# Block softmax: the running maximum's scan between the slot's last two block sums, and GpSimd's low parts subtracted in two halves

## The reference, cut to what matters

```python
def step(carry, kv):
    o, m, l = carry
    kj, vj = kv
    s = jnp.einsum('bhnqd,bhkd->bhnqk', qb, kj) * scale
    m_new = jnp.maximum(m, s.max(axis=-1))
    p = jnp.exp(s - m_new[..., None])
    alpha = jnp.exp(m - m_new)
    l_new = alpha * l + p.sum(axis=-1)
    o_new = (alpha[..., None] * o + jnp.einsum('bhnqk,bhkd->bhnqd', p, vj)) / l_new[..., None]
    return ((o_new, m_new, l_new), None)
```

## Time and profile before

| what | value |
|---|---|
| median of 3 runs | 2512.51 us |
| lowest, highest | 2512.49, 2518.15 us |
| the profiled execution: span from first to last instruction | 2524.1 us |
| TensorE busy | 2303.2 us (91%) |
| VectorE busy | 2215.7 us (88%) |
| ScalarE busy | 1658.7 us (66%) |
| GpSimd busy | 1477.1 us (59%) |

### The profile page before, as it was taken

One profiled execution on the slowest core, in us unless ns is written; L12 is line 12 of the kernel. 1 busy time (PEld: TensorE's weight loads), 2 busy tenths in 40 slices (PEclk: granted clock), 3 DMA queues, 4 the chain that ended last, 5 costly groups with the idle time before them and its releaser, 6 DMA issues. The chain is left out here.

```text
span 2524.1 us, 44143 instructions
## 1 busy us (share of the span) xinstructions
PE 2303.2 (91%) x14954; PEld 1763.9 (70%) x14954; DVE 2215.7 (88%) x4723; ACT 1658.7 (66%) x2901; POOL 1477.1 (59%) x1073
## 2 busy tenths in 40 slices
PE   5996699659999999999999999999999999957995
PEld 3553588537777777777777777777777777746884
DVE  6675688789999999999999999999999999956886
ACT  2464344367777777787877778777777887733443
POOL 1145344336667666667667767666876766653442
PEclk8997799879999999999999999999999999978997
DMA  8811566564344533444223332233322333006665
GB/s 202 228 63 49 172 211 208 170 167 118 85 97 102 131 94 84 101 112 105 63 62 87 92 86 62 62 79 79 99 71 63 79 86 72 5 27 190 205 212 187
DMA packets 169680, 281.89 MB, mean 112 GB/s; under 512 B 32972, under 2 KB 122962, under 8 KB 169456
## 3 DMA queue, kind: packets, MB, share of 16 engines
q1 hardware_dynamic: 160240, 260.11, 39.9%
q0 software_dynamic: 9216, 18.96, 2.2%
HBM read 118.94 MB, written 62.39 MB: 72 GB/s over the span
## 5 line engine op out<-in xcount | busy, mean ns | idle before, releaser
L2628 POOL TENSOR_TENSOR b_prob<-b_prob,b_weight 128x1024 f32<-128x1024 f32 x512 | 958.4, 1903 | 501.9 <-DVE b_weight L2585 501.2
L2555 DVE TENSOR_REDUCE b_bmax<-b_score 128x16 f32<-128x1024 f32 x512 | 621.5, 1214 | 44.8 <-PE b_score L2405 31.0
L2507 ACT ACTIVATE b_prob<-b_score,b_neg_m 128x1024 f32<-128x1024 f32 x512 | 581.1, 1135 | 75.1 <-DVE b_neg_m L2563 73.4
L2492 ACT ACTIVATE b_pT<-b_turn 128x512 f32<-128x512 f32 x1024 | 560.6, 609 | 70.2 <-PE b_turn L2418 62.7
L2542 DVE TENSOR_REDUCE b_bsum<-b_prob 128x16 f32<-128x1024 f32 x512 | 605.6, 1202 | 0.0
L2418 PE MATMUL b_turn<-ident,b_prob 128*128 128x128 f32 x4096 | 533.1, 273 | 4.7 <-ACT b_pT L2492 3.3
L2418 PEld LDWEIGHTS b_turn<-ident,b_prob 128*128 128x128 f32 x4096 | 478.6, 141 | 76.5 <-ACT b_pT L2492 4.2
L2405 PE MATMUL b_score<-b_KH,b_QS 128*128 128x512 f32 x1024 | 476.6, 465 | 21.2 <-ACT b_prob L2507 15.5
L2386 PE MATMUL b_acc<-b_pT,b_V 128*64 128x256 f32 x4096 | 470.3, 382 | 0.0
L2405 PE MATMUL b_score<-b_KL,b_QS 128*128 128x512 f32 x1024 | 406.0, 396 | 0.0
L2386 PEld LDWEIGHTS b_acc<-b_pT,b_V 128*64 128x64 f32 x4096 | 282.8, 137 | 150.7 <-issue 21.4
(11 more groups left out here) (349 smaller groups left out, 2947.3 us busy)
## 6 DMA issues: line engine op xcount, KB each, us to landing
f_e_w<-f_weights SPq DMA_DIRECT2D x80, 776.0 KB
f_sorted<-zeros SPq DMA_DIRECT2D x172, 193.5 KB, 6.0
b_KH<-b_k_high SPq DMA_DIRECT2D x128, 256.0 KB, 4.2
b_KL<-b_k_low SPq DMA_DIRECT2D x128, 256.0 KB, 4.6
b_QS<-b_q_high SPq DMA_DIRECT2D x64, 256.0 KB, 3.8
b_QS<-b_q_low SPq DMA_DIRECT2D x64, 256.0 KB, 3.6
b_hb<-b_hT SPq DMA_DIRECT2D x31, 512.0 KB, 5.1
f_e_z<-f_sorted SPq DMA_DIRECT2D x62, 129.0 KB
```

The source lines that it names most:

```text
L2492: act.activation(pT(g, k)[h][:], turn[h][:], ACT.Copy).then_inc(evac, 1)
L2507: act.activation(prob[r % 4][k][:], score[k % 2][:], ACT.Exp, bias=neg_m[r % 2][:, k:k + 1]).then_inc(prob_ready, 1)
L2555: maxima = chain.mark(dve.tensor_reduce(bmax[r % 2][:, k, :], score[k % 2][:].rearrange("p (n c) -> p n c", c=KV_BLOCK), AX, ALU.max))
L2628: pool.tensor_tensor(tile, tile, weight[r % 2][:, k, :].unsqueeze(2).to_broadcast([P, NB, KV_BLOCK]), ALU.mult).then_inc(scaled, 1)
```

## The change

At k=0 the scan of the running maximum moves from before both block sums to between them. The scan of the running sum moves ahead of the addition on the running maximum, and the reciprocal waits for it by its own mark. On GpSimd, each low part (128 x 512) is subtracted by two instructions of 128 x 256; the semaphore is raised by the second.

```diff
                         if k == 0 and rest:
+                            block_sums(n, nr, GT - 2)
                             m_i = chain.mark(dve.tensor_tensor_scan(flat(run_max), flat(first_low), flat(bmax[nr % 2]), 0.0, ALU.add, ALU.max))
-                            block_sums(n, nr, GT - 2)
                             block_sums(n, nr, GT - 1)
+                            dve.wait_ge(sum_ready, 4 * n + 4)
+                            l_i = chain.mark(dve.tensor_tensor_scan(flat(run_sum), flat(first_least), flat(bsum[nr % 2]), 1.0, ALU.mult, ALU.add))
                             chain.wait(m_i)
                             dve.tensor_tensor(run_max[:], run_max[:], neg_m[nr % 2][:].unsqueeze(2).to_broadcast([P, GT, NB]), ALU.add).then_inc(gap_ready, 1)
-                            dve.wait_ge(sum_ready, 4 * n + 4)
-                            chain.link(dve.tensor_tensor_scan(flat(run_sum), flat(first_least), flat(bsum[nr % 2]), 1.0, ALU.mult, ALU.add))
+                            chain.wait(l_i)
                             inverse = chain.mark(dve.reciprocal(flat(inv_l), flat(run_sum)))
...
                     pool.wait_ge(high_ready, 4 * i + u + 1)
-                    pool.tensor_tensor(whole, whole.bitcast(F32), high.bitcast(F32), ALU.subtract).then_inc(qk_taken, 1)
+                    for first in (0, HALF // 2):
+                        cut = slice(first, first + HALF // 2)
+                        last = pool.tensor_tensor(whole[:, cut], whole[:, cut].bitcast(F32), high[:, cut].bitcast(F32), ALU.subtract)
+                    last.then_inc(qk_taken, 1)
```

## The result

The changed kernel takes 2502.77 us (median of 7 runs) against 2511.82 (7 runs) for the kernel before, measured beside it: ratio 0.9964, 95% interval 0.9952 to 0.9975, **9 us or 0.36% faster**. A second comparison (experiment 5) gave 2500.4 against 2510.2, ratio 0.9963 (0.9950 to 0.9976). The sign was right, the size half of what was forecast.

The account below looks back on a forecast made before the run. TensorE was busy 91% and VectorE 88%, with VectorE's scan stalls behind GpSimd reaching TensorE. Waits for oT (−13) and late exponentials (−7) gave −20 us, taken from the run median: 2492.5, stated as 2493; range 2486 to 2516.

Parts of the forecast that it names:

- Part 1: At k=0, block softmax: the maximum's scan, moved between the sums, saves VectorE 0.89 us in the V (value-projecting) slot.
- The 0.33: Microseconds TensorE loses in a V slot, its step before the output projection taking 1.20 against 0.87; forecast as won.
- the sum: Forecast total: oT waits −13, late exponentials −7, together −20 us: profiled span 2524.1 to 2504, run median 2493.
- Late exponentials: Disturbed slots, TensorE waiting for ScalarE's exponentials: of some 10 us, a VectorE burst shorter by 0.9 per slot takes 7.
- Part 1's condition: Without low parts, the moved scan finds GpSimd done if the last weighing ends under 1.12 us behind the old start.
- Part 2: Running sum's scan ahead of the addition on VectorE: 0.13 us saved, the addition covering the wait on the chain.
- Part 3: GpSimd low parts in halves: a half taken as 0.9 us, a low part growing from 1.28 to about 1.8, nothing late.
- Part 4: Halves meeting VectorE: if the addition slips in, maximum at 3.83 us, scores at 4.25; K and N slots lose nothing.
- rival A: Addition locked out by GpSimd halves, undisturbed rounds only: +14, V and Q slots −15, net −1, 2511 us; chance 0.22.
- rival B: Same addition lock in all 32 N slots once a half costs 0.95 or more: +16, 2528 us; chance 0.13.
- Rival C: V slot's TensorE idles for something else at once, the turned copies: only −3, 2509 us; chance 0.07.

Follow-up runs that it names:

- experiment 5: The changed kernel again, unedited, on another chip: 2500.4 us against 2510.2 for the kernel before, ratio 0.9963.
- experiment 10: The change with gain and shift in four pieces, plus GpSimd waiting behind its scatters in slots 64, 68, 96, 100: 2493.6 us against 2510.6 for the kernel before.
- experiments 3 and 4: 3: the change, scan at its old place in the ten slots, ratio 0.9927; 4: the change, sorter's gain and shift in four instructions each, ratio 0.9932.
- experiment 6: The change with gain and shift in four pieces, plus the first two units' scatters spread over six slots instead of four: 2491.05 us, ratio 0.9924.
- experiments 1 and 8: 1: the change with low parts whole (new order alone), ratio 0.9959; 8: the same with gain and shift in four pieces, ratio 0.9948.
- experiment 2: The kernel before with only the low parts halved, VectorE in the old order: ratio 1.0045, slower by 11 us.
- experiment 7: Separate bench without attention and experts: 90 trials, VectorE's scan moved against four GpSimd halves; scan at most 0.9 us in 71 of 72 trials without the weighing.
- experiment 9: Separate bench: chains of up to four scatters, four weighings and four halves, 84 trials in six kinds; no scan above 0.92 us.

## Why the forecast was half right

- **Part 1, the V slot: right.** The 0.33 was won (step 1.20 to 0.87); an undisturbed V slot went from 12.61 to 12.22. V slots outside the ten gained 13.6 us; the sum had 13. That the two agree is in part luck, since the sum counted TensorE's waits for oT, and these did not fall from 28 to a few: they went from 12.2 us in 28 waits to 14.1 in 18. The 16 short ones of the V slots are gone, but those in N slots and slot 128 stayed (3.0 and 2.6 us) and the ten slots brought 8.6 of new ones. Each undisturbed V slot gained 0.39, not 0.33.
- **Late exponentials: right in direction, the size not shown.** Disturbed Q, K and N slots gained 7.3; the sum had 7. But 1.7 of the 7.3 is that of slots 64, 68, 96 and 100 (experiment 10), which leaves 5.7. ScalarE's exponentials waited for VectorE's negated maximum for 71.1 us in 124 waits before and 40.3 in 94 after, which is the mechanism; that the slots' gain is this and nothing else no run shows. Outside the ten slots and those four, the gain is 19.2, near the forecast's 20.
- **Part 1's condition is the step that failed.** It said that the scan, moved 1.12 later, "without low parts" finds GpSimd done if the last weighing has ended, and priced its worst case from the weighing alone. But GpSimd's program has other instructions behind the weighing: the sorter's gain and shift, 2.19 us each, in slots 47, 48, 79, 80, 111 and 112, where the old place was the better one. L905's duration stood in the earlier trace rows, used there for the price of a half only. This costs 5.3 us; experiments 3 and 4 take 4.4 of it away by two ways. In 65, 69, 97 and 101 the low parts follow a weighing that scatters made late, and the scan is shut out through all four: these slots lose 4.9 us, with the slots ahead of them 3.2 net. Against experiment 5, the pairs are 4.5 shorter in experiment 6 and 3.0 in experiment 10, where the pause alone was added. No row of before showed a block over several instructions, since its longest scan was 1.56. With both cured (experiment 6) the time is 19 below the kernel before, near the sum, though up to 1.2 of that may be the spreading's own.
- **Part 2, mostly missing:** the three short instructions come 0.13 faster (0.32 from the scan of the sums to the reciprocal, 0.45 in the earlier trace rows), but they start 1.23 behind the last sum's start where 1.12 was counted: 0.02 net. The V slot's scores were ready all the same.
- **Part 3, a term mis-sized:** a half takes 0.73, not 0.9. Halves follow each other at 0.69. By the rate that the GPSIMD Engine Reference of the Trainium skill gives (section 3.1, about 2.6 cycles an element), with what a whole low part took beyond it, the estimate was 0.72; the trace agrees, and I was wrong to price a half by L684, whose rows are 1024 wide.
- **Part 4, wrong in its mechanism, right in its result:** the addition does not slip in, it is locked out for the fourth half (0.69 in K and N slots), as in rival A. With halves of 0.73 it is over before the scores come. Rival A had the lock right and its price wrong, because it used ends 0.86 to 0.93 apart; rival B needed pieces of 0.95. Rival C is refuted by the V slot.
- **Where the halves pay:** by the traces of one chip 2.2 to 2.5 us in disturbed slots, over half of it in N slots, with a gain or a loss of under 1 us more behind the scatters, and nothing in undisturbed rounds (experiments 1 and 8); by the times it is not resolved. Alone they cost 11 us (experiment 2). They belong with the new order.

## What to carry to other kernels

When a two-input VectorE instruction is moved past other work to miss a GpSimd instruction, list what GpSimd runs at the new time in every slot, the riders that come in a few slots only too: three pairs of slots with a 2.19 us instruction and four behind scatters took back about half of this gain. Cutting GpSimd's long instructions into pieces bounds what a badly timed one costs, at some 0.15 us for each cut here (four halves 2.83 against 2.51 for two whole parts, the gain 2.62 in four pieces against 2.19), and the pieces should be tried against every two-input instruction near them, since alone they made this kernel slower. Leave GpSimd a pause behind a run of scatters. Before two traces are compared slot by slot, compare stretches that the change doesn't touch, and look which chip each stems from.

## What the runs showed of the hardware

- A two-input VectorE instruction that meets a running GpSimd one gets in at that one's end, though the next GpSimd instruction is recorded from 0.03 to 0.06 before that end. A held-up scan ends 0.14 to 0.17 us behind it (experiment 7 and the kernels' scans), 0.15 to 0.21 in experiment 9, the shorter addition 0.08 (K and N slots). In 71 of the 72 trials of experiment 7 without the weighing no scan was held by more than one piece. SBUF — State Buffer of the Trainium skill (Who interferes with whom) has the wait for the whole instruction; the trace agrees, and adds that, but for the exception below, a chain of instructions is no longer an obstacle than the one that was met.
- An instruction that starts a little behind the recorded start of a GpSimd one is shut out for all of it: the scan of the sums 0.08 to 0.11 behind in experiment 1 (1.31 to 1.35 us, nine slots), the addition 0.15 to 0.18 behind after (0.68 to 0.70).
- The exception: behind scatters and four weighings with next to no pause between them, the scan waits for the end of the whole chain. Slots 65, 69, 97 and 101 of the ten traces of the kernel give 40 cases. In 23 GpSimd paused for 0.25 us or more between scatter and weighing, and the scan was let in at the next end in every one (slot 65 before: pause 0.26, scan 0.61). In 17 the pause was 0.05 or less, and the scan waited for the chain's end in 16, up to 2.67 us, and 3.16 in experiment 3; slot 101 of experiment 3 (pause 0.05, scan 0.45) is the one against. Slot 128 had a pause of 0.03 or less in all ten traces: the scan waited for the end of the weighings (2.54 to 2.55) in eight, and was let in at the next end (1.04, 1.06) in the two with the old order. So a pause ends the block, but its absence alone doesn't make it, and the same chain by itself doesn't show it (experiment 9). What else it takes stays open.
